# Forgetting recurrence, second quantised feed-forward part and damped recurrence, run as one pipeline over the batches

## The chip, the core and the metric

The kernel runs on one core of one Trainium2 chip. The metric is the device time of that core in microseconds. A core has a matrix engine (TensorE, PE in the profile; its weight loads are the row PEld), a vector engine (VectorE, DVE), an activation engine (ScalarE, ACT), a general engine (GpSimd, POOL) and a queue that issues transfers (SyncE, SP). Each engine works through its own list of instructions in order and waits on semaphores for the others.

## The reference

The residual stream x has 2048 tokens of 128 channels. The whole network is a row of residual parts, `x = x + part(layernorm(x))`; the three that the change touches stand in its middle:

```python
# the forgetting recurrence (batch s of the kernel is one step of the scan, 16 heads of 8)
f = sigmoid(x @ Wf.T + bf);  phi = elu(.) + 1
S = f * S + phi_k (x) v;  z = f * z + phi_k
out = (phi_q . S) / (phi_q . z + 1e-6) @ Wo.T + bo

# the quantised part: blocks of 16 along the last axis are rounded to a 4-bit grid
gate, up = fp4_linear(x, w_gate), fp4_linear(x, w_up)      # 128 -> 352
h = silu(gate) * up
out = fp4_linear(h, w_down)                                # 352 -> 128

# the damped recurrence: a causal filter over the batches, c = gamma * exp(i * theta)
y[n] = real(sum_m c^(n-m) x[m] + last * c^(n+1));  out = y * x
```

Ahead of them stand a latent attention and a first quantised part; behind them four layers of local attention with a gated feed-forward part, two on either side of a gated linear attention.

## The kernel before, in words

The tokens are held in SBUF for the whole run, X (the residual stream) and XH (its normalised copy), as 8 batches (NB) of 2 tiles (NT) of 128 tokens by 128 channels. A plan names the stages in order, `norm0, attn_a, ffn4, forget, ffn4, conv, win, mlp, ...`, and every engine's program walks the plan stage by stage and the batches inside a stage. Semaphores count the events; `v.at(name, i, k)` is the count of event k of batch i in the stage v.

In each stage the last step of a batch on DVE is `residual` (L779: add to X, L782, then the statistics in `norm_stats`, L634), then POOL raises var to the power -1/2 (`rstd_of_batch`, L516 and L518), and DVE writes XH in `norm_apply` (L645).

The recurrence (`forget`): POOL copies XH of the next batch to xst (`stage_copy`, L520), a batch ahead of the rstd that it computes in the same loop (L584 to L591). PE transposes xst (`transpose_x`, L1838), ACT copies the transpose to xT (L1219), PE projects it with a one-row bias matmul and a full one for each tile (`forget_pe`, L1818, banks 0 and 1), ACT takes exp, relu and values out of PSUM (`forget_act`, L1285, signal c_act), and DVE does the step (`forget_step`, L836; L841 is its first instruction, for each tile), whose operands grow with the batch number, since all earlier keys and values are kept and weighted anew. PE transposes the result yC and projects it (`forget_out`, L1826). DVE does step s and then the residual and the normalisation of batch s-1.

The second quantised part (`ffn4`): DVE quantises the hidden values of batch i together with the input of batch i+2 in one interleaved chain (`ffn4_quantise`, L815), PE transposes and multiplies (`ffn4_gates`, L1770, gate and up of both tiles into banks 0 to 3), ACT computes silu (L1272), DVE the product (`ffn4_h`, L826), and PE the down projection (`ffn4`, L1782, bank 7, lines L1788 and L1794). The middle batches are in a hardware loop.

The damped recurrence (`conv`): PE transposes XH (L1801), adds up the taps over all earlier batches in PSUM (`conv_taps`, L1798, banks 0 and 1 in turn), and DVE multiplies by XH and adds to X (`conv_step`, L876). Its end is interleaved with the opening of the first window stage (`win_open`, L921 on DVE), which ends, for this document, at the first instruction of L1576 on PE. POOL clears the buffer keysZ (L514) at the beginning of this stage.

Of the kernel before, what the change touches and what calls it, by code (L numbers as in the profile page):

```python
# [26 lines left out]
P = 128  # L27
NB = 8
# [57 lines left out]
AHEAD = ("forget", "lin")  # L86


def attn_unit(u, groups):


    if u < groups:
# [23 lines left out]
        "stage_ready": 1, "xT_psum": 1, "xT_ready": 1, "c_proj": NT, "c_act": NT, "c_y": 1,  # L116
# [27 lines left out]
             "forget": ["xT_ready", "c_act", "yT_ready", "down_used"], "conv": ["xT_ready", "down_used"],  # L144
# [11 lines left out]
           "pv_done": 2, "o_used": 1, "h_ready": 2, "down_used": 1, "hqT_psum": 1,  # L156
           "shift_done": 16, "p_used": 4, "phi_done": 2, "lin_st": 3, "lin_av": 2, "lin_y": 2}
NAMES = sorted({n for c in COUNTS.values() for n in c})


class Val:


    def __init__(self, sems, plan, at_stage):
        self.sems, self.counts = sems, COUNTS[plan[at_stage]]
        self.base = {n: CREDITS.get(n, 0) + NB * sum(COUNTS[k].get(n, 0) for k in plan[:at_stage])
                     for n in NAMES}

    def at(self, name, i, k):

        assert self.base[name] + k > 0 or (isinstance(i, int) and i * self.counts[name] + self.base[name] + k > 0), (name, k)
        return i * self.counts.get(name, 0) + self.base[name] + k
# [6 lines left out]
class Chain:  # L179
# [6 lines left out]
    def mark(self, ins):  # L186
        self.n += 1
        ins.then_inc(self.val.sems[self.name], 1)
        return self.n

    def wait(self, n):
        self.eng.wait_ge(self.val.sems[self.name], self.val.at(self.name, self.i, n))
# [4 lines left out]
    def close(self, want=None):  # L197
        if want is None:
            want = self.val.counts.get(self.name, 0)
# [3 lines left out]
def build(nc, x, out, consts, w, plan):  # L203
    with ExitStack() as ctx:
# [13 lines left out]
        def carve(name, members):  # L218
# [26 lines left out]
            [("t1", [NT, 2 * FH * FHD]), ("t2", [NT, 2 * FH * FHD]), ("convp", [NT, C])], [("eG", [2, 512]), ("rG", [2, 512]), ("yG", [NT, LH * LHD])]])  # L245
# [21 lines left out]
        hrstd = sb("hrstd", [P, NT])  # L267
        scratch = sb("scratch", [P, 1])
# [18 lines left out]

        ckvZ = tmp["ckvZ"]
# [31 lines left out]
        xhT = tmp["xhT"]; convp = tmp["convp"]  # L320
# [49 lines left out]
        vals = [Val(sems, plan, n) for n in range(len(plan))]  # L370

# [6 lines left out]
        def opens(n):  # L378

            return plan[n] == "conv" and plan[n + 1:n + 2] == ["win"]  # L380

# [22 lines left out]
        def _(sp):  # L404
# [7 lines left out]
            for n, kind in enumerate(plan):  # L412
                if kind == "conv":

                    sp.wait_ge(sems["xh_ready"], vals[n - 2].at("xh_ready", NB - 1, 1))
# [23 lines left out]
        def _(pool):  # L439
# [68 lines left out]
            for n, kind in enumerate(plan):  # L508
# [3 lines left out]
                if kind == "conv":  # L512
# [3 lines left out]
                def rstd_of_batch(i):  # L516
                    pool.wait_ge(sems["var_ready"], v.at("var_ready", i, 1))
                    pool.tensor_tensor(rstd[:], var[:], mhalf[:, 0:NT], ALU.pow).then_inc(sems["rstd_ready"], 1)  # L518

                def stage_copy(i, n=n):  # L520
                    ready = ANNOUNCES.get(plan[n - 1], "xh_ready")
                    pool.wait_ge(sems[ready], vals[n - 1].at(ready, i, 1))
# [45 lines left out]
                if kind == "attn_a":  # L568
# [14 lines left out]
                    continue  # L583
                if kind in AHEAD:  # L584

# [6 lines left out]
                if kind == "win":  # L592

                    pool.wait_ge(sems["xh_ready"], v.before("xh_ready"))
# [20 lines left out]
                if opens(n):  # L615
                    for i in range(2):
                        rstd_of_batch(i)
                    stage_copy(0, n + 1)
                    with pool.Fori(2, NB - 1) as i:
                        rstd_of_batch(i)  # L620
                    inverse_norms(vals[n + 1], 0, 0)
                    rstd_of_batch(NB - 1)
                    continue
# [5 lines left out]
        def _(dve):  # L629
# [4 lines left out]
            def norm_stats(v, i, ch):  # L634

                settle()
                marks = [ch.mark(dve.bn_stats(stats[:, t], X[:, i, t])) for t in range(NT)]
                ch.wait(marks[-1])
                settle()
                for t in range(NT):  # L640
                    m = ch.mark(dve.bn_aggr(mv[:, t], stats[:, t]))
# [1419 lines left out]
```

## Time and profile before

| | |
|---|---|
| median of 3 runs | 2079.46 us (2076.47 to 2080.57) |
| the profiled execution | 2078.81 us, its span 2076.7 us |
| mean granted clock of PE | 0.912 |
| PE busy | 1755.0 us (85%) |
| DVE busy | 1393.1 us (67%) |
| ACT busy | 936.7 us (45%) |
| POOL busy | 453.3 us (22%) |

The span is from the first to the last instruction; the rest of the time lies around it. A share of busy time is a mean over stages that have different limits, so the stretch that the change touches is read by itself. The granted clock is given as a share of 2.4 GHz, and 0.5 is 1.2 GHz. "Idle before" names how long an engine stood and what ended that.

### The profile page before, as it was taken

The numbers are of one execution on the slowest core, as the hardware profiler recorded it, in microseconds if no ns is written. First come the engines' busy times: TensorE is split into PE (matmuls) and PEld (weight loads), VectorE is DVE, ScalarE is ACT, GpSimd is POOL, SyncE is SP. The second block draws the span as 40 slices with busy tenths as digits, with TensorE's granted clock in tenths as the row PEclk, the third lists the DMA queues.
The fourth block names the chain that finished last, engine by engine and source line by source line (L and its number), as shares of the span: only waits on it lengthen the run. The fifth ranks groups of instructions, "written<-read, shape, count | busy, mean of one in ns | idle before, by whom it ended". The sixth has DMA issues, their size and how long they took to land.

```text
span 2076.7 us, 34010 instructions
## 1 busy us (share of the span) xinstructions
PE 1755.0 (85%) x10875; PEld 1415.7 (68%) x10875; DVE 1393.1 (67%) x3623; ACT 936.7 (45%) x2557; POOL 453.3 (22%) x352
## 2 busy tenths in 40 slices
PE   6999986654467699999989789999987999999997
PEld 5888874422246477777777667787775777777776
DVE  4556579646698677787787655566446777777774
ACT  3444432211121456656656445344404566566654
POOL 2200010000001343343343200000003433433440
PEclk9999987655588899999999999999968999999999
DMA  3000000000100000000000000000000000000000
GB/s 138 0 0 0 0 1 0 0 0 0 50 0 1 1 4 3 3 2 3 3 1 3 3 1 0 0 0 0 0 1 0 4 3 3 2 3 3 1 2 23
DMA packets 15104, 13.76 MB, mean 7 GB/s; under 512 B 11286, under 2 KB 14138, under 8 KB 14650
## 3 DMA queue, kind: packets, MB, share of 16 engines
q1 hardware_dynamic: 15034, 12.88, 1.9%
q8 instruction: 37, 0.61, 0.1%
q14 instruction: 33, 0.27, 0.0%
HBM read 9.74 MB, written 1.05 MB: 5 GB/s over the span
## 4 chain that ended last, share of the span: by engine, by line
PE 39%; issue 31%; DVE 24%; ACT 4%; POOL 2%; DVEq 1%; POOLq 0%; ACTq 0%
PE bank L1530 5%; PE bank L1661 3%; DVE arena_ffn L903 3%; DVE arena_attn L918 3%; PE bank L1562 3%; PE bank L1699 3%; DVE ssq L911 3%; PE bank L1550 3%; PE bank L1648 3%; DVE arena_ffn L899 2%; DVE probT L688 2%; PE bank L1724 2%; PE bank L1703 2%; PE bank L1541 2%; DVE nmaxF L681 2%
## 5 line engine op out<-in xcount | busy, mean ns | idle before, releaser
L534 POOL TENSOR_TENSOR arena_ffn<-arena_ffn 128x1024 f32<-128x1024 f32 x60 | 141.3, 2356 | 503.1 <-DVE arena_ffn L903 503.1
L518 POOL TENSOR_TENSOR rstd<-var,mhalf 128x2 f32<-128x2 f32 x48 | 33.4, 695 | 901.2 <-DVE var L643 901.2
L688 DVE COPY probT<-bank 128x512 f32<-128x512 f32 x288 | 196.9, 684 | 25.6 <-PE bank L1541 25.5
L530 POOL TENSOR_TENSOR inv<-ssq,mhalf 128x16 f32<-128x16 f32 x64 | 186.2, 2910 | 69.7 <-DVE ssq L912 69.4
L1550 PE MATMUL bank<-vF,probT 128*128 128x64 f32 x1536 | 195.9, 271 | 5.8 <-DVE probT L688 4.3
L1550 PEld LDWEIGHTS bank<-vF,probT 128*128 128x128 f32 x1536 | 186.5, 192 | 12.8 <-DVE probT L688 12.5
L681 DVE TENSOR_REDUCE nmaxF<-bank 128x2 f32<-128x384 f32 (+1 forms) x192 | 114.8, 598 | 90.1 <-PE bank L1530 89.7
L1530 PE MATMUL bank<-arena_setup 128*128 128x192 f32 (+1 forms) x1024 | 173.0, 302 | 0.0
L1530 PEld LDWEIGHTS bank<-arena_setup 128*128 128x128 f32 x1024 | 155.8, 193 | 12.5 <-issue 1.1
L1371 ACT ACTIVATE arena_conv<-bank,nmaxF 128x192 f32<-128x192 f32 x256 | 105.4, 419 | 115.9 <-DVE nmaxF L681 112.5
L1253 ACT ACTIVATE prob<-bank,nmax 128x128 f32<-128x128 f32 (+1 forms) x256 | 88.7, 428 | 125.0 <-DVE nmax L681 125.0
L1562 PE MATMUL bank<-packF,hT 128*128 128x512 f32 x256 | 123.3, 606 | 1.8 <-ACT hT L1305 1.8
L681 DVE TENSOR_REDUCE nmax<-bank 128x2 f32<-128x512 f32 (+1 forms) x96 | 65.1, 689 | 66.2 <-PE bank L1530 66.2
L1661 PE MATMUL bank<-xT,w1s 128*114 128x256 f32 (+1 forms) x384 | 103.8, 397 | 3.3 <-ACT xT L1352 1.1
L1330 ACT ACTIVATE arena_setup<-bank 128x512 f32<-128x512 f32 x64 | 38.1, 595 | 151.2 <-PE bank L1610 150.7
L1541 PE MATMUL bank<-ident,prob 128*128 128x128 f32 x640 | 96.8, 274 | 9.4 <-ACT prob L1253 9.3
L1310 ACT ACTIVATE arena_attn<-bank 128x512 f32<-128x512 f32 x128 | 69.6, 601 | 74.6 <-PE bank L1562 74.6
L1054 DVE TENSOR_TENSOR arena_forget<-bank,maskG 128x384 f32<-128x384 f32 x128 | 68.2, 552 | 50.4 <-PE bank L1726 47.4
L1530 PE MATMUL bank<-arena_attn 128*128 128x256 f32 (+1 forms) x512 | 99.3, 326 | 0.0
L1219 ACT ACTIVATE xT<-bank 128x256 f32<-128x256 f32 x40 | 15.3, 383 | 183.9 <-PE bank L1841 130.2
L903 DVE TENSOR_TENSOR arena_ffn<-bank,rope 128x256 f32<-128x256 f32 x256 | 95.5, 415 | 0.0
L1576 PE MATMUL bank<-packF,hT 128*128 128x512 f32 x128 | 73.6, 662 | 24.5 <-DVE arena_ffn L903 24.5
(257 smaller groups left out, 4262.4 us busy)
## 6 DMA issues: line engine op xcount, KB each, us to landing
packF<-in_packF SPq DMA_DIRECT2D x1, 3122.0 KB
arena_history<-in_packG SPq DMA_DIRECT2D x1, 2560.0 KB, 9.1
HS<-XH SPq DMA_DIRECT2D x32, 63.5 KB
X<-in_x_tiled SPq DMA_DIRECT2D x1, 1024.0 KB, 4.9
out_dram<-X SPq DMA_DIRECT2D x8, 128.0 KB, 1.9
arena_setup<-in_const_masks_a SPq DMA_DIRECT2D x1, 512.0 KB, 5.4
arena_setup<-in_const_masks_f SPq DMA_DIRECT2D x1, 512.0 KB
HS<-XH SPq DMA_DIRECT2D x32, 0.2 KB
```

The lines of the kernel that those rows point to most:

```text
L530: pool.tensor_tensor(inv[:, t, :, 0], ssq[:, t, :, 0], mhalf[:, 0:16], ALU.pow).then_inc(sems["inv_ready"], 1)
L534: pool.tensor_tensor(t1[:, t], t1[:, t], t2[:, t], ALU.add).then_inc(sems["rope_sum"], 1)
L681: dve.tensor_reduce(out_[:, u, 0:heads], bank[u % banks][:, 0:heads * keys].rearrange("p (h k) -> p h k", k=keys), AX.X, ALU.max, negate=T ...
L688: dve.tensor_copy(probT[:, u % 2], bank[4 + u % 2][:]).then_inc(sems["pt_copied"], 1)
L903: ins = dve.tensor_tensor(heads(t2[:, t, cols])[:, :, d], a[:, :, e], tab, ALU.mult)
L1253: ins = act.activation(prob[:, u % 2, m * keys:(m + 1) * keys], bank[u % 4][:, m * keys:(m + 1) * keys], ACT.Exp, bias=nmax[:, u, m:m + 1])
L1371: ins = act.activation((prob, probW)[t][:, u % 2, (k + 1) * keys - width:(k + 1) * keys], bank[u % F_SCORE_BANKS][:, k * width:(k + 1) * w ...
L1530: ins = pe.matmul(bank[s % banks][:, n * width:(n + 1) * width], q, k, start=False, stop=True, skip_group_check=True)
L1541: ins = pe.transpose(bank[4 + u % 2][:, n * P:(n + 1) * P], pr[:, u % 2, n * P:(n + 1) * P], ident[:])
L1550: ins = pe.matmul(o, probT[:, u % 2, n * P:(n + 1) * P], val, start=first, stop=(kt == keys // P - 1), skip_group_check=True)
L1562: ins = pe.matmul(bank[banks[m]][:], hT[:, t * P:(t + 1) * P], f_at[f"wqkv{l}"][:, 512 * m:512 * m + 512], start=True, stop=True)
L1661: return pe.matmul(dst, w1s[:, l, lo:lo + n], xT[:], start=True, stop=True)
```

## The change

The three stages `forget`, `ffn4` (the second one) and `conv` become one loop of NB+3 turns, written out, on each engine. In turn k the recurrence works on batch k, the quantised part (now called `q`, with its own semaphores) quantises the hidden values of batch k-2 together with the input of batch k-1, and the damped recurrence does batch k-3. PE and ACT do the projections of the recurrence one batch ahead (k+1). Each of the three has its own tiles for the statistics (the table `moments`). PE transposes XH itself, without POOL's copy. The PSUM banks are shared out anew: 0 and 1 projections, 2 both transposes of the recurrence (by halves), 3 the taps, 4 the transposes of q and conv (by halves), 5 and 6 gate, then up in the same bank after silu has read it, and the transposes of hq, 7 the two outputs (by halves). ACT changes between the tables of Exp and Silu in every turn (`prime`). The memset of keysZ moves to the beginning of `forget`. The core of the diff:

```diff
-AHEAD = ("forget", "lin")
+AHEAD = ("lin",)
-    plan = ["norm0", "attn_a", "ffn4", "forget", "ffn4", "conv"] + local + ["lin"] + local
+    plan = ["norm0", "attn_a", "ffn4", "forget", "q", "conv"] + local + ["lin"] + local
...
 # POOL
+                if kind == "forget":
+                    vq, vc = vals[n + 1:n + 3]
+                    for k in range(NB + 3):
+                        if k < NB:
+                            rstd_of_batch(k)
+                        if k == NB + 2:
+                            inverse_norms(vals[n + 3], 0, 0)
+                        if inside(k - 3) is not None:
+                            rstd_of_batch(k - 3, vc)
+                        if k == NB:
+                            stage_copy(0, n + 3)
+                        if inside(k - 2) is not None:
+                            rstd_of_batch(k - 2, vq)
+                    continue
...
 # DVE
+                    for k in range(NB + 4):
+                        if k < NB:
+                            forget_step(vf, k)
+                        q_quantise(vq, vf, inside(k - 2), inside(k - 1))
+                        if k < NB:
+                            forget_end(vf, k)
+                        if k == NB + 2:
+                            win_open(vals[n + 3], 0, 0)
+                        if inside(k - 3) is not None:
+                            conv_step(vc, k - 3)
+                        if inside(k - 2) is not None:
+                            q_end(vq, k - 2)
+                        if k < NB:
+                            norm_apply(vf, k)
+                        if inside(k - 3) is not None:
+                            norm_apply(vc, k - 3)
+                        if inside(k - 2) is not None:
+                            norm_apply(vq, k - 2)
+                        if inside(k - 1) is not None:
+                            q_h(vq, k - 1)
+                    win_open(vals[n + 3], 0, 1)
...
 # ACT
+                    forget_act(v, 0)
+                    for k in range(NB + 3):
+                        if inside(k - 3) is not None:
+                            take_tokens(vc, k - 3)
+                        if k + 1 < NB:
+                            forget_act(v, k + 1)
+                        if k < NB:
+                            forget_yT(v, k)
+                        if inside(k - 2) is not None:
+                            q_hqT(vq, k - 2)
+                        if inside(k - 1) is not None:
+                            prime(ACT.Silu)
+                            q_take_xT(vq, k - 1)
+                            q_silu(vq, k - 1)
+                            prime(ACT.Exp, 1)
+                    win_open(vals[n + 3])
...
 # PE
+            def q_out(v, i, vf):
+                pe.wait_ge(v.sem("hq_ready"), v.at("hq_ready", i, 1))
+                for t in range(NT):
+                    for n in range(NCH):
+                        ins = pe.transpose(bank[5 + t][:, n * P:(n + 1) * P], hq[:, t, n * P:(n + 1) * P], ident[:])
+                    ins.then_inc(v.sem("hqT_psum"), 1)
+                if i + 2 < NB:
+
+                    pe.wait_ge(vf.sem("down_used"), vf.at("down_used", i + 2, 1))
+                elif i:
+                    pe.wait_ge(v.sem("down_used"), v.at("down_used", i, 0))
...
+            def q_gates(v, i):
+                pe.wait_ge(v.sem("xq_ready"), v.at("xq_ready", i, 1))
+                for t in range(NT):
+                    ins = pe.transpose(bank[4][:, t * P:(t + 1) * P], xq[:, t * P:(t + 1) * P], ident[:])
+                ins.then_inc(v.sem("xT_psum"), 1)
+                pe.wait_ge(v.sem("xT_ready"), v.at("xT_ready", i, 1))
+                for m, done in enumerate(("gate_ready", "up_ready")):
+                    for t in range(NT):
+                        if m:
+                            pe.wait_ge(v.sem("silu_ready"), v.at("silu_ready", i, t + 1))
+                        pe.matmul(bank[5 + t][:, 0:FI], xqT[:, t * P:(t + 1) * P], wguT[:, m, 0:FI], start=True,
+                                  stop=True).then_inc(v.sem(done), 1)
...
+                    forget_pe(v, 0, vals[n - 1])
+                    for k in range(NB + 3):
+                        if inside(k - 3) is not None:
+                            conv_taps(vc, k - 3, vq)
+                        if k + 1 < NB:
+                            forget_pe(v, k + 1, vals[n - 1])
+                        if k < NB:
+                            forget_out(v, k)
+                        if inside(k - 2) is not None:
+                            q_out(vq, k - 2, v)
+                        if inside(k - 1) is not None:
+                            q_gates(vq, k - 1)
+                    win_open(vals[n + 3], 0)
```

In `forget_pe` and `forget_out` the first bias matmul now stands ahead of the wait for ACT's copy.

## Rows read from the trace of the kernel before

**Rows 1.** Windows: time, then busy of PE, PEld, DVE, ACT, POOL; clock, DMA.
```profile
397.00:555.90 158.90, 85.01 (x160) 37.78 (x160) 89.57 (x217) 21.04 (x81) 8.33 (x16) 0.50 0.00 0
555.90:652.70 96.80, 59.27 (x230) 42.72 (x230) 88.80 (x264) 20.05 (x49) 4.85 (x7) 0.76 0.07 27
...
397.00:691.80 294.80, 169.63 (x587) 102.99 (x587) 206.99 (x588) 46.84 (x143) 28.33 (x38) 0.64 0.02 9
```

**Rows 2.** Waits of DVE from 397.0 to 691.8: total us, times, longest.
```profile
DVE arena_forget L841 <- ACT cEf L1295: 57.9, 16, 5.2
DVE XH L649 <- POOL rstd L518: 9.7, 12, 0.8
```

**Rows 3.** Timeline (start, us, engine, line), last step of the recurrence.
```profile
526.59 0.48 PE L1840 MATMUL bank<-ident,xst 128*128 128x128 f32 x1 [11.82 <-POOL xst L526]
...
532.05 0.29 DVE L841 SCALAR_TENSOR_TENSOR arena_forget<-arena_forget 128x128 f32<-128x128 f32 x1 [5.18 <-ACT cEf L1295]
...
535.32 0.29 DVE L841 SCALAR_TENSOR_TENSOR arena_forget<-arena_forget 128x128 f32<-128x128 f32 x1 [2.68 <-ACT cEf L1295]
...
549.17 0.41 DVE L782 TENSOR_TENSOR X<-X,bank 128x256 f32<-128x256 f32 x1
549.31 0.69 PE L1829 MATMUL bank<-ident,arena_forget 128*128 128x128 f32 x2 [10.74 <-DVE arena_forget L867]
...
553.47 0.42 DVE L782 TENSOR_TENSOR X<-X,bank 128x256 f32<-128x256 f32 x1 [1.46 <-PE bank L1835]
```

**Rows 4.** Timeline, seam into the recurrence and its second step.
```profile
394.77 0.42 DVE L782 TENSOR_TENSOR X<-X,bank 128x256 f32<-128x256 f32 x1 [1.81 <-PE bank L1794]
...
397.47 0.31 PE L1840 MATMUL bank<-ident,xst 128*128 128x128 f32 x1 [2.73 <-POOL xst L526]
...
402.61 0.29 DVE L841 SCALAR_TENSOR_TENSOR arena_forget<-arena_forget 128x128 f32<-128x128 f32 x1 [4.95 <-ACT cEf L1295]
...
413.73 0.29 DVE L841 SCALAR_TENSOR_TENSOR arena_forget<-arena_forget 128x128 f32<-128x128 f32 x1 [2.68 <-ACT cEf L1295]
...
419.06 0.42 DVE L782 TENSOR_TENSOR X<-X,bank 128x256 f32<-128x256 f32 x1
```

**Rows 5.** Timeline, two turns of the second quantised part.
```profile
619.89 0.89 DVE L725 TENSOR_REDUCE amax<-arena_ffn 128x44 f32<-128x704 f32 x1
...
621.47 2.63 PE L1779 MATMUL bank<-wguT,xT 128*128 128x352 f32 x8 [0.56 <-ACT xT L1219]
...
627.82 0.42 DVE L782 TENSOR_TENSOR X<-X,bank 128x256 f32 x1
...
629.10 2.93 PE L1794 MATMUL bank<-wdT,arena_ffn 128*128 128x128 f32 x12
...
630.66 0.88 DVE L725 TENSOR_REDUCE amax<-arena_ffn 128x44 f32<-128x704 f32 x1
...
633.02 4.78 PE L1779 MATMUL bank<-wguT,xT 128*128 128x352 f32 x8 [0.56 <-ACT xT L1219]
...
637.26 0.41 DVE L782 TENSOR_TENSOR X<-X,bank 128x256 f32<-128x256 f32 x1
```

**Rows 6.** Timeline, damped recurrence and opening of the window stage.
```profile
653.38 1.81 POOL L514 MEMSET arena_setup<- 128x2048 f32 x1
...
655.26 0.40 DVE L880 TENSOR_TENSOR arena_ffn<-bank,XH 128x256 f32<-128x256 f32 x1
...
657.04 0.42 DVE L880 TENSOR_TENSOR arena_ffn<-bank,XH 128x256 f32<-128x256 f32 x1
...
670.09 0.38 PE L1801 MATMUL bank<-ident,XH 128*128 128x128 f32 x2
...
674.22 0.14 PEld L1840 LDWEIGHTS bank<-ident,xst 128*128 128x128 f32 x1
...
691.79 1.19 PE L1576 MATMUL bank<-packF,hT 128*128 128x512 f32 x1 [12.53 <-DVE arena_ffn L903]
```

**Rows 7.** ACT's table loads by line: busy us, mean ns, idle before.
```profile
L1266 ACT ACT_TABLE_LOAD x58 | 74.4, 1283 | 1.0
```

More of the change, by code:

```diff
@@ L829, in ffn4_h, with q_h, q_quantise, q_end @@
                     dve.tensor_tensor(h[:, t], silu[:, t], bank[2 * t + 1][:, 0:FI], ALU.mult).then_inc(sems["h_ready"], 1)
+            def q_h(v, i):
+                for t in range(NT):
+                    dve.wait_ge(v.sem("up_ready"), v.at("up_ready", i, t + 1))
+                    dve.tensor_tensor(h[:, t], silu[:, t], bank[5 + t][:, 0:FI], ALU.mult).then_inc(v.sem("h_ready"), 1)
+            def q_quantise(v, vin, hi, xi):
+                jobs = ([h_job(v, hi)] if hi is not None else []) + ([x_job(v, xi, vin)] if xi is not None else [])
+                if not jobs:
+                    return
+                ch = Chain(dve, v, "quant_chain", 0, q_quantise.links)
+                last = quantise(jobs, ch.mark, ch.wait)
+                q_quantise.links = ch.n
+                if xi is not None:
+                    last.pop().then_inc(v.sem("xq_ready"), 1)
+                if hi is not None:
+                    last.pop().then_inc(v.sem("hq_ready"), 1)
+            q_quantise.links = 0
+            def q_end(v, i):
+                ch = Chain(dve, v, "dve_chain", i)
+                residual(v, i, ch, bank[7][:, 0:T])
+                ch.close()
             def ffn4_end(v, i):
@@ L1298, in forget_yT @@
                 act.wait_ge(sems["yT_psum"], v.at("yT_psum", s, 1))
-                act.activation(yT[:], bank[2][:, 0:T], ACT.Copy).then_inc(sems["yT_ready"], 1)
+                act.activation(yT[:], bank[2][:, T:2 * T], ACT.Copy).then_inc(sems["yT_ready"], 1)
             def shifted(v, i, b=2):
@@ L1796, in ffn4 @@
                 ins.then_inc(sems["down_ready"], 1)
+            def q_out(v, i, vf):
+                pe.wait_ge(v.sem("hq_ready"), v.at("hq_ready", i, 1))
+                for t in range(NT):
+                    for n in range(NCH):
[5 more added lines that the diff above has]
+                    pe.wait_ge(v.sem("down_used"), v.at("down_used", i, 0))
+                for t in range(NT):
+                    pe.wait_ge(v.sem("hqT_ready"), v.at("hqT_ready", i, t + 1))
+                    for n in range(NCH):
+                        ins = pe.matmul(bank[7][:, t * P:(t + 1) * P], hqT[:, t, n], wdT[:, n],
+                                        start=(n == 0), stop=(n == NCH - 1))
+                ins.then_inc(v.sem("down_ready"), 1)
@@ L1807, in conv_taps @@
+                ins.then_inc(v.sem("xT_psum"), 1)
+                if i:
+                    pe.wait_ge(v.sem("down_used"), v.at("down_used", i, 0))
+                y = bank[3]
                 for t in range(NT):
@@ L1902, in _ @@
                 v = vals[n]
-                if kind.startswith("mlp") or kind == "win" and not begins(n):
+                if kind.startswith("mlp") or kind in ("q", "conv") or kind == "win" and not begins(n):
                     continue
```

195 lines of the change are left out of this document (93 added, 102 removed).

## The prediction

> **What bounds the kernel now.** I read the page first, then the stretch that the change touches as windows [rows 1], then what VectorE (DVE) waits for in it [rows 2], then one turn of each of the three stages as a timeline. The stretch runs from 397.0 to 691.8 us: 294.8 us, of which DVE is busy 207.0 and PE 169.6. No engine is full. In the forgetting recurrence (158.9 us) DVE is busy 89.6, and in the quantised part (96.8 us) 88.8 [rows 1]: the second is bound by DVE, the first by a wait. That wait has one row: DVE stood 57.9 us, 16 times, before L841, for the last of ScalarE's (ACT) reads of the projections [rows 2]. The timeline says why. The transposes of batch 7 start at 526.59, after 11.82 us of waiting for GpSimd's (POOL) copy xst, though XH of that batch is far older: the copy stands in POOL's queue behind the square root of batch 5. L841 then starts 5.46 us later for the first half and 3.27 us later again for the second [rows 3]. The other waits are 9.7 us for POOL's rstd [rows 2] and single stalls at the seams. PE is granted half of its clock (1.2 GHz) through the whole recurrence, 0.76 on average in the quantised part [rows 1].
>
> **The change, part by part.** I follow DVE, because in the new order each engine's queue is a fixed list of turns k, and DVE has the most work. Its turn is: recurrence step k, joint quantisation (hidden of batch k-2, input of k-1), residual of the recurrence k, damped step k-3, residual of the quantised part k-2, three normalisations, gating products k-1.
>
> Prices. (a) Recurrence step: batch 1 from 413.73 to 419.06 [rows 4], batch 7 from 535.32 to 549.17 [rows 3], each plus 0.59 for its first half: 5.9 and 14.4, growing by 1.42 a batch, so 58.0 for batches 3 to 7 and 7.3 for batch 2. (b) Joint quantisation: 619.89 to 627.82, 7.9. Hidden alone: 630.66 to 637.26, 6.6 [rows 5]. (c) Residual with statistics 1.45 (its six instructions follow one another), damped step 655.26 to 657.04, 1.8 [rows 6]; one normalisation 0.53; gating products 0.95. (d) rstd on POOL 0.9 with its hop: it stalled 12 times for 9.7 [rows 2].
>
> Removed: POOL's copy and its semaphore on the path to the transposes; PE now transposes XH itself, and the projections of k+1 are issued a turn ahead, during step k. So the 57.9 us should shrink to the first batch. They need PE for about 1.3 us and four matmul groups of 1.63 (two of them are the 3.27 us of rows 3), 7.9 us at half clock, behind the taps of k-3. A step is 8.8 us or more from k=3 on and PE starts 0.6 us before it, so the taps of batch 0 (six matmuls, about 2 us) and the projections end at about the time the step ends; the later, longer taps meet longer steps. What queues behind them is the output of the recurrence. That one takes 4.2 us from the last product to the residual (549.25 to 553.47 [rows 3]), 3.6 now that its bias matmul goes ahead of ACT's copy, and it lies beside the 7.9 us of quantisation. Late next is therefore not L841 but the end of the turn.
>
> Let T be the end of the joint quantisation. DVE's own work after it is 1.45+1.8+1.45+1.6+0.95, so the turn could end at T+7.2. But the quantised part's output needs PE: after the quantisation ended at 627.82 its down projection ran from 629.10 for 2.93 us at the lower clock [rows 5], so the residual can start at T+4.3, where DVE would be at T+3.25. PE's gates k-1 stand behind it: transposes and ACT's copy, 0.9 us at full clock or 1.3 at half (5.46 less 3.27 less 0.9 for ACT's reads), then four matmuls of 352 columns, 2.63 us at full clock or 4.78 at half [rows 5], 0.3 for hops and the silu, 0.5 for the last product. That gives T+8.6 with the projection at the lower clock and the gates at the higher one, T+7.2 all high (then DVE itself is the bound), T+11.2 all low. I take 8.6: after a down projection at the lower clock the gates ran in 2.63 us four times of five in the trace, in 4.78 once; one of each stands in [rows 5].
>
> Added on ACT: a table load before each Silu and before each Exp of the next turn, 17 instead of 2. One takes 1.28 us, and 58 of them elsewhere in this kernel had 1.0 us of idle time before them in all [rows 7]. Silu's load runs from about T+1.9 to T+3.4 (T+1.2 to T+2.7 at full clock), and the transposes that it must not delay end at T+5.2 or T+3.3. Exp's load lies beside taps and transposes. I cost them at nothing; if the cover were gone, one load per turn is 1.28 x 8 = 10 us. The Trainium skill, ScalarE: Activation LUTs, "What ACT_TABLE_LOAD costs", adds a drain of 1380 ns to 1283 ns per switch, and its section on table sets advises to batch calls by set, which speaks against this change; with 2.66 us in each of eight turns the sum would be 21 us worse. The trace agrees with the 1283 ns, not with a drain.
>
> Moved at no cost: the memset of keysZ, 1.81 us on POOL [rows 6], now at the start of the stretch, where DVE waits anyway (it can lengthen one normalisation beside it that nobody waits for). SP's load of packG is issued when the recurrence's last batch is normalised, as before, and is needed stages later. The unrolled q turns replace loops; nothing in the trace prices that, and the recurrence, already unrolled, shows no fetch stall, so zero, bounds -3 to +3 us.
>
> **The sum**, in times of the trace before.
> - k=0: PE waited for xst until 397.47; the residual that it must wait for ends at 395.2 [rows 4]. The first L841 moves from 402.6 to 400.4, the second half to 403.7, the step ends at 407.6. The projections of batch 1 (four groups, 6.5) stand ahead of output 0: 410.2, output 413.8, residual, rstd, normalisation: 416.7.
> - k=1: +5.9 = 422.6; output 3.6 = 426.2 (input quantisation, 16 blocks of 60, is shorter); gates at half clock 1.3+4.8+0.3+0.5 = 433.1.
> - k=2: +7.3+7.9+8.6 = 456.9.
> - k=3 to 7: 58.0+5x16.5 = 597.6.
> - k=8: 16.5 = 614.1. k=9: 6.6, then down projection 4.5, residual 1.45, rstd 0.9, normalisation 0.5 = 628.1.
> - Tail: the taps of batch 7 now start only here: 670.09 to 674.22 is 4.1 us at full clock [rows 6], 8.2 at half, I take 5.5. From 674.22 to 691.79 the opening of the window stage is unchanged, 17.6 us. Ends at 651.3.
> That is 40.5 us earlier than 691.8. The profiled execution took 2078.8 us (span 2076.7 and 2.1 around it), 0.7 below the median of the three; 2078.8-40.5 = 2038.3.
>
> **The rivals.**
> - PE stays at half clock, as in the whole recurrence before [rows 1], whose bursts of 7 us did not lift it: 2.6 us more in k=2 to 8, 4 us in the tail: +22, 2060. For it: the same projections, with one-row bias matmuls, are in every turn. Against: the clock rose in the quantised part with less PE work per time.
> - PE at full clock through: -1.4 in seven turns, -3 in k=1, -3 in k=9 and tail: -16, 2022. Against it: PE idles from the output k to T.
> - The table loads are in the chain: +10 us by the row, 2049, up to 2060 where two stand in a turn. By the page's price it would be 2059.
> - Slower than before: the in-order queues expose what I hide. If step k+1 found its projections not done (8.7 us from transposes to the second L841 [rows 3]) and output k was exposed too (3.6), a turn costs 12.3 more, seven turns 86: 2124. It decides from half of the turns on (40.5/12.3 = 3.3). It would take PE's queue running a turn behind DVE's; in my sum PE is ahead by only a fraction of a microsecond at k=3.
> - It doesn't do what it says: smaller new waits (POOL, bank 7 shared by two outputs, gates) of 5 to 6 us in each of seven turns eat the gain: about 2078.
>
> **How the numbers follow.** Chances: forecast 0.50 (2029 to 2048), half clock 0.20, full clock 0.15, table loads 0.05, slower 0.06, no change 0.04. The range 2018 to 2066 takes the first four with the bounds of the unrolled code and of clock changes in later stages (some us either way). Faster 0.90, within 0.2% (4 us, about what a measurement of this kernel can tell from no change) 0.03, slower 0.07.
>
> **What would show it.** Right: L841's idle time under 10 us; L782 of the quantised part waiting about 1 us a turn for the down projection and the last product about 0.3 us for PE; turns from k=3 of 25 to 31 us; the window stage unchanged, 40 us earlier. Wrong: idle time before L841 from k=2 on, the recurrence's residual waiting in turns after k=1, ACT's loads naming themselves as releasers, or a stretch in which DVE is busy under 75%.

## The result and the profile after

The changed kernel took 2022.28 us (median of four runs, 2020.02 to 2022.44), the kernel before, in runs on the same chip, 2080.02 us (2076.47 to 2084.73). The ratio is 0.9719, with an interval of 0.9698 to 0.9739: 58 us faster, where 40.5 was forecast. The profiled execution took 2022.21 us (span 2020.4), 56.6 less than the one of before.

Of these I first look for the part that lies in the stretch. Windows of the kernel after (time, then busy of PE, PEld, DVE, ACT, POOL; clock, DMA): the whole stretch, up to the first instruction of L1656, which was L1576.

```profile
395.00:645.90 250.90, 155.69 (x586) 100.42 (x587) 204.90 (x596) 68.87 (x167) 26.38 (x31) 0.70 0.03 11
```

The kernel before, from 395.00 as well ([rows 1] starts it at 397.00):

```profile
395.00:691.80 296.80, 169.63 (x587) 102.99 (x587) 208.08 (x596) 46.84 (x143) 29.05 (x39) 0.64 0.02 9
```

DVE runs 596 instructions in both. They keep it busy for 208.08 of 296.80 us (70%) before and for 204.90 of 250.90 us (82%) after. The stretch ends 45.9 us earlier (645.9 against 691.8; forecast 651.3).

Waits of DVE from 395 to 645.9, kernel after (total us, times, longest). L894 was L841, L811 was L782, L678 was L649; L1892 is the down projection of q, L1952 the output of the recurrence, L1906 the gates.

```profile
DVE X L811 <- PE bank L1892: 12.3, 8, 2.9
DVE ssq L961 <- ACT arena_attn L1383: 10.4, 1, 10.4
DVE X L811 <- PE bank L1952: 6.0, 1, 6.0
DVE arena_ffn L863 <- PE bank L1906: 3.3, 4, 2.0
DVE XH L678 <- POOL rstd L539: 2.4, 3, 0.8
DVE arena_forget L894 <- ACT cEf L1368: 2.3, 1, 2.3
```

The row of 57.9 us in [rows 2] has become one of 2.3. In its place stand the down projection of the quantised part (eight waits, 12.3 us) and one wait for the output of the recurrence in the first turn.

A turn in the middle shows where these lie. Timeline of the kernel after (start, us, engine, line), from the last part of recurrence step 6 (turn k=6) to the start of step 7:

```profile
544.99 0.88 DVE L754 TENSOR_REDUCE amax<-arena_ffn 128x44 f32<-128x704 f32 x1
...
546.46 0.80 PE L1952 MATMUL bank<-woTb,yT 128*128 128x128 f32 x2
...
552.70 1.54 PE L1882 MATMUL bank<-ident,hq 128*128 128x128 f32 x6 [3.99 <-DVE hq L802]
552.90 0.41 DVE L811 TENSOR_TENSOR X<-X,bank 128x256 f32<-128x256 f32 x1
...
554.27 2.90 PE L1892 MATMUL bank<-wdT,arena_ffn 128*128 128x128 f32 x12
...
554.79 1.28 ACT L1339 ACT_TABLE_LOAD   x1
...
556.08 0.20 ACT L1339 ACTIVATE primer<-mhalf 128x1 f32<-128x1 f32 x1
...
557.21 0.42 DVE L811 TENSOR_TENSOR X<-X,bank 128x256 f32<-128x256 f32 x1 [1.09 <-PE bank L1892]
...
558.07 3.03 PE L1906 MATMUL bank<-wguT,xqT 128*128 128x352 f32 x8 [0.47 <-ACT xqT L1281]
...
560.20 1.28 ACT L1339 ACT_TABLE_LOAD   x1
560.54 1.11 DVE L863 TENSOR_TENSOR arena_ffn<-arena_ffn,bank 128x352 f32<-128x352 f32 x2 [0.37 <-PE bank L1906]
561.57 0.28 DVE L894 SCALAR_TENSOR_TENSOR arena_forget<-arena_forget 128x128 f32<-128x128 f32 x1
```

The joint quantisation starts at 544.99 and the recurrence's residual follows it at 552.90 without a wait; its output on PE was done long before. From there to the next step (561.57) DVE waits 1.09 us for the down projection and 0.37 us for the last gate product. Both table loads lie beside PE's work and nobody names them. The other turns from k=3 to k=7 look alike; the wait for the down projection is 0.51 us in turn 3 and 0.91 to 1.10 us in turns 4 to 7. It is longer in turn 2 (2.89 us) and where DVE has less to do beside it, in turns 8 and 9 (2.42 and 2.33 us).

The stretch gives 45.9 us and the whole 56.3 (spans). The other 10.4 lie far behind it. I cut both spans at the same instructions: the start of the last batch of gated linear attention (first score matmul, L1724 before, L1804 after) and its last output matmul (L1766, L1846).

| part of the span, us | before | after | difference |
|---|---|---|---|
| to the end of the stretch | 691.8 | 645.9 | -45.9 |
| window stages and gated linear attention, up to its last batch | 815.35 | 821.59 | +6.2 |
| last batch of gated linear attention | 42.85 | 30.21 | -12.6 |
| the rest | 526.7 | 522.7 | -4.0 |

The windows of that batch, before and after:

```profile
1507.00:1550.00 43.00, 39.52 (x209) 35.48 (x209) 19.04 (x74) 2.35 (x4) 0.69 (x1) 0.60 0.00 1
```
```profile
1467.00:1498.00 31.00, 26.73 (x214) 23.90 (x212) 18.94 (x74) 2.39 (x4) 0.70 (x1) 0.94 0.01 1
```

The same instructions (74 on DVE in both), and PE at a mean clock of 0.60 in one and 0.94 in the other. The change doesn't touch the source of this batch. The timeline of before shows where the clock fell; the same group of four takes 0.70 us at first and 1.23 in the last row:

```profile
1507.15 0.70 PE L1724 MATMUL bank<-arena_setup 64*128 64x256 f32 x4
...
1509.51 0.70 PE L1724 MATMUL bank<-arena_setup 64*128 64x256 f32 x4 [1.43 <-DVE arena_forget L1054]
...
1511.08 0.52 PE L1747 MATMUL bank<-vG,arena_forget 128*128 128x65 f32 x2
...
1512.38 1.23 PE L1724 MATMUL bank<-arena_setup 64*128 64x256 f32 x4
```

It falls from 2.4 to 1.2 GHz at about 1511, 1.6 us after the end of a hole of 1.43 us, and stays there for 34 us, in which PE is busy 96% of the time:

```profile
1511.00:1545.00 34.00, 32.64 (x154) 29.36 (x153) 15.65 (x62) 1.19 (x2) 0.00 (x0) 0.50 0.00 1
```

In the kernel after the same hole is there (1.43 us, ending at 1469.84), and the groups behind it still take 0.70 us.

### The profile page after: what moved, and what is told of

Its sections match the earlier page's. It is cut to its first block, busy times and chain, and to the rows that moved or that the text cites. A ratio compares the mean times of both kernels' runs of the same rounds, so it can differ in the third digit from the quotient of the medians.

```text
span 2020.4 us, 33580 instructions
## 1 busy us (share of the span) xinstructions
PE 1724.9 (85%) x10818; PEld 1403.6 (69%) x10875; DVE 1389.0 (69%) x3623; ACT 957.3 (47%) x2580; POOL 450.6 (22%) x344
## 4 chain that ended last, share of the span: by engine, by line
PE 43%; DVE 33%; issue 18%; ACT 4%; POOL 1%; DVEq 1%; POOLq 0%; ACTq 0%
PE bank L1610 5%; PE bank L1741 4%; DVE arena_ffn L953 3%; DVE arena_attn L968 3%; PE bank L1779 3%; PE bank L1642 3%; DVE ssq L961 3%; PE bank L1728 3%; PE bank L1630 3%; DVE arena_ffn L949 3%; DVE probT L717 2%; PE bank L1783 2%; PE bank L1804 2%; DVE nmaxF L710 2%; PE bank L1621 2%
## 5 line engine op out<-in xcount | busy, mean ns | idle before, releaser
L539 POOL TENSOR_TENSOR rstd<-var,mhalf 128x2 f32<-128x2 f32 x32 | 22.3, 696 | 796.5 <-DVE var L672 796.5
L1610 PEld LDWEIGHTS bank<-arena_setup 128*128 128x128 f32 x1024 | 154.3, 191 | 12.3 <-issue 1.0
L1339 ACT ACT_TABLE_LOAD x74 | 94.9, 1283 | 1.3
L1656 PE MATMUL bank<-packF,hT 128*128 128x512 f32 x128 | 73.3, 659 | 25.1 <-DVE arena_ffn L953 25.1
```

The costliest lines, as they stand in the source:

```text
L1339: act.activation(primer[:, col:col + 1], mhalf[:, 0:1], func)
L1610: ins = pe.matmul(bank[s % banks][:, n * width:(n + 1) * width], q, k, start=False, stop=True, skip_group_check=True)
```

## The experiments

Two questions are open: what in the stretch brought the 45.9 us, the pipeline or a part of it; and whether the other 10 us belong to the change. "Stretch end" and "batch" below are the first and third row of the table above, for the profiled execution. The same code of the stretch, profiled again in a kernel that differs only behind it, ended it at 691.5 to 691.8 in the order of before (before, e5, e10), at 644.1 to 646.1 in the changed order (after, e6, e11), at 644.2 and 645.1 in e1 and e7, and at 636.5 and 634.6 in e4 and e8. So a difference of up to 2 us between two stretch ends is not read as an effect.

**e1: the copy alone.** The kernel before, three stages one after the other, with PE transposing XH itself in `forget`:

```diff
-AHEAD = ("forget", "lin")
+AHEAD = ("lin",)
...
-            def forget_pe(v, s):
-                transpose_stage(v, s, bank[6])
+            def forget_pe(v, s, vin):
+                pe.wait_ge(sems["xh_ready"], vin.at("xh_ready", s, 1))
+                for t in range(NT):
+                    ins = pe.transpose(bank[6][:, t * P:(t + 1) * P], XH[:, s, t], ident[:])
+                ins.then_inc(sems["xT_psum"], 1)
+                pe.wait_ge(sems["xT_ready"], v.at("xT_ready", s, 1))
...
```

> The kernel before with one edit: TensorE transposes XH itself in the recurrence, without GpSimd's copy; the three stages still follow one another. Theory A (the copy behind the square root is what cost the time, and the pipeline over the three stages adds little): the projections of batch s+1 stand behind output s-1 and take 4.2 + 8.7 = 13 us from the last product of s-1, VectorE's step s and its residual take 8.8 to 17 us, so waits of about 4, 3 and 1 us stay at the first steps, some 16 us before L841 in all instead of 57.9; the stretch takes 250 to 255 us instead of 294.8, the kernel 2036 to 2040. Theory B (the pipeline is what hides them): L841 still waits 30 us or more, the kernel takes 2050 or more.

Measured: 2031.44 us, ratio 0.9783 (0.9767 to 0.9799). Theory A holds, with more gain than it gave: L841 waits 11.5 us where 16 were expected, and the time is 5 us below its range. Windows of the recurrence and of the stretch, and DVE's waits:

```profile
397.00:555.00 158.00, 109.01 (x261) 55.85 (x260) 131.29 (x344) 30.70 (x105) 6.93 (x10) 0.58 0.05 17
397.00:644.20 247.20, 165.27 (x584) 101.67 (x583) 205.87 (x588) 45.94 (x142) 25.51 (x30) 0.66 0.03 11
```
```profile
DVE arena_forget L841 <- ACT cEf L1295: 11.5, 7, 2.7
DVE XH L649 <- POOL rstd L518: 9.7, 12, 0.8
DVE ssq L911 <- ACT arena_attn L1310: 6.0, 1, 6.0
DVE arena_ffn L829 <- ACT arena_ffn L1272: 2.6, 2, 1.6
```

The stretch ends at 644.2, that of the whole pipeline at 645.9: the same within the scatter. The order of before already issues the projections of batch s+1 ahead of the output of batch s; only POOL's copy, queued behind an older rstd, held them back. The trace of before shows it ahead of the last step:

```profile
525.50 0.69 POOL L518 TENSOR_TENSOR rstd<-var,mhalf 128x2 f32<-128x2 f32 x1 [22.77 <-DVE var L643]
526.14 0.40 POOL L526 COPY xst<-XH 128x256 f32 x1
```

POOL stood idle for 22.77 us, waiting for the statistics of batch 5; the copy of batch 7, 0.40 us long, stood behind it, though its input had been there for nearly all of that time. With it gone, DVE is busy 131.29 of 158.00 us (83%) in the recurrence, against 89.57 of 158.90 (56%) in [rows 1], with the stages still one after the other. The pipeline hides more of the rstd (9.7 becomes 4.2 in all) and of the projections (11.5 becomes 2.3), and pays with the down projection (12.3), the first output (6.0) and a longer wait at the seam into the window stage (10.4 for 6.0).

**e2: projections in their own turn.** The changed kernel, but in turn k PE and ACT do the projections of batch k, not k+1:

```diff
-                    forget_pe(v, 0, vals[n - 1])
...
-                        if k + 1 < NB:
-                            forget_pe(v, k + 1, vals[n - 1])
+                        if k < NB:
+                            forget_pe(v, k, vals[n - 1])
```

(the same for `forget_act`).

> The changed kernel with the recurrence's projections and ScalarE's reads of them in the turn of their batch instead of one turn ahead. By the price of the rival in the prediction (12.3 us a turn, seven turns at half clock) 86 us more, 2108; if TensorE holds its full clock behind the gates and the taps, 5 us for the projections and the taps of 2 to 3 us ahead of them, 8 us a turn, 55 more, 2077. If running ahead were of no use: 2022.

Measured: 2070.3 us (2050.84 to 2076.8), ratio 0.9942 (0.991 to 0.9974); stretch end 682.3, 36.4 later than in the changed kernel.

```profile
DVE arena_forget L894 <- ACT cEf L1368: 39.6, 15, 5.3
```

This row is 37.3 us more than the 2.3 of before the edit. The first output waits 2.3 us less (3.7 for 6.0) and the seam 1.0 us more (11.4 for 10.4), so this one wait explains the 36.4 us. In this profile the pipeline without the projections run ahead keeps 9.5 of the 45.9 us. The eight runs scatter over 26 us and the profiled one is the slowest of them, so another run may have kept more; even the fastest is only 26 us below the kernel before on its chip, where the changed kernel is 58 us below. The expectation of 86 us at the lower clock was too high; the one of 55 us more, at the full clock (2077), is near the profiled 2076.8. But that total has 12.6 us of the later batch in it, and the stretch had 36.4. So what carries most of the gain is that the projections are issued during the step ahead, in either order.

**e3: no table changes.** Silu replaced by a plain copy and both `prime` calls left out in the loop, so that the part computes gate times up, not silu(gate) times up, with 16 table loads fewer.

```diff
-                    act.activation(silu[:, t], bank[5 + t][:, 0:FI], ACT.Silu).then_inc(v.sem("silu_ready"), 1)
+                    act.activation(silu[:, t], bank[5 + t][:, 0:FI], ACT.Copy).then_inc(v.sem("silu_ready"), 1)
...
-                            prime(ACT.Silu)
...
-                            prime(ACT.Exp, 1)
```

> The changed kernel with Silu replaced by a plain copy and both table changes of each turn left out: the quantised part computes gate * up instead of silu(gate) * up, everything else is as it was, and 16 table loads of 1.28 us are gone. Loads hidden, as in the sum of the prediction: 2020 to 2023, no change. Loads in the chain (one or two a turn): 10 to 21 us faster, 2001 to 2012.

Loads by line (busy us, mean ns, idle before), first the changed kernel, then this one:

```profile
L1339 ACT ACT_TABLE_LOAD x74 | 94.9, 1283 | 1.3
```
```profile
L1339 ACT ACT_TABLE_LOAD x58 | 74.4, 1283 | 1.0
```

Measured: stretch end 645.7 against 645.9. Without sixteen loads, 20.5 us of ACT's time, the stretch ends 0.2 us sooner, which is inside the scatter of 2 us, where the rival had 10 to 21 us: they are hidden. The Trainium skill's page ScalarE: Activation LUTs, section "What ACT_TABLE_LOAD costs", has 1283 ns for the load, as here; its drain of 1380 ns on top, which was a rival, shows in no row: in the turn above the load ends at 556.07 and ACT's next instruction starts at 556.08. And yet the time was 2035.73 us (2035.7, 2035.76, 2037.02, and one of 2021.32), 13 us slower than the changed kernel. Of the 13.6 us between the profiled spans 12.6 are the batch of gated linear attention:

```profile
1465.00:1508.00 43.00, 39.52 (x210) 35.47 (x209) 19.03 (x74) 2.32 (x4) 0.70 (x1) 0.60 0.00 1
```

It took 42.84 us here, as before the change, and in e1 42.86. Two kernels whose stretches end within 0.2 us of each other differ by 12.6 us in a batch 800 us later. That answers half of the second question: the pipeline alone does not bring those us, since e3 has it and runs this batch at the lower clock (so does e2, at a mean of 0.60).

**e4: a higher clock in the pipeline.** Matmuls whose result nobody reads (256 columns, into bank 4), on PE while it waits for the recurrence step or for the quantisation:

```diff
+            def fill(n):
+                for _ in range(n):
+                    pe.matmul(bank[4][:, 0:T], ident[:], wC[:, 0:T], start=True, stop=True)
...
+                        if 3 <= k < NB:
+                            fill((6, 8, 10, 12, 20)[k - 3])
                         if k < NB:
                             forget_out(v, k)
+                        if k > 2 and inside(k - 2) is not None:
+                            fill(6)
                         if inside(k - 2) is not None:
                             q_out(vq, k - 2, v)
```

> The changed kernel with idle TensorE time filled by matmuls of 256 columns whose result nobody reads: 6 to 20 of them while the recurrence's step runs on VectorE (turns 3 to 7) and 6 between its output and that of the quantised part. If the lower clock of the down projection costs about 1.1 us a turn (the wait before the residual), that wait goes and turns 3 to 9 get 1 to 1.5 us shorter: 2012 to 2016. If VectorE is the bound anyway: 2022. If the fillers run at the lower clock they stand in the way, 1 us each instead of 0.5: 2025 to 2040.

```profile
395.00:636.50 241.50, 189.88 (x783) 128.24 (x783) 203.78 (x596) 68.33 (x167) 26.42 (x31) 0.82 0.03 12
```

The clock of the stretch rose from 0.70 to 0.82 and its end moved from 645.9 to 636.5. The 9.4 us lie in what the expectation had for seven shorter turns (7 to 10.5). The time is 2017.87 us in the median, but the four runs are two pairs, 2009 and 2027 to 2028; the profiled one is a 2009, and its batch ran at a mean clock of 0.89 (from 1453 to 1485). A comparison to a few us needed the later batch to be held still.

**e5 to e8: the batch held at the higher clock.** Three such matmuls in the last batch of gated linear attention, early in it, where PE otherwise falls to half:

```diff
+                    if not more and s == 2:
+                        pe.wait_ge(sems["p_used"], v.at("p_used", i, 16))
+                        for _ in range(3):
+                            pe.matmul(bank[0][:, 0:T], ident[:], wC[:, 0:T], start=True, stop=True)
```

in the kernel before (e5), the changed one (e6), e1 (e7) and e4 (e8), all on one chip, where the kernel before took 2080.80 us.

> The kernel before with three matmuls of 256 columns (result read by nobody, 1.5 us at full clock) in the 1.4 us in which TensorE waits between the first and the second pair of heads of the last batch of the gated linear attention. In the trace before, that batch took 42.9 us at the lower clock, in the trace after 30.2 us at the full one. Theory C (10 of the 56 us of the change were this batch's clock, which falls or not in that hole, and have nothing to do with the pipeline): the batch takes 30 to 31 us, the kernel 2063 to 2066 in every run instead of 2076. Theory D (the clock there follows from something else, the hole isn't its cause): 2076 to 2081 as before.

> The changed kernel with the same three matmuls. Theory C: the batch had kept its clock there already in this kernel's runs, so nothing changes: 2020 to 2024, and the gain against the kernel before with the same matmuls is the 45.9 us of the stretch alone, or less. Theory D: the difference stays at 56 us.

> The three stages one after another, TensorE transposing XH itself (one edit to the kernel before), with the same three matmuls. Its stretch ended at 644.2, that of the changed kernel at 645.9, but its last batch of the gated linear attention took 42.9 us. Theory C: 2031.4 less 12 = 2019 to 2020, as fast as the whole pipeline with the hold or 1 to 2 us faster. Theory D: 2031 as before.

> The changed kernel with filled TensorE time in the pipeline's turns (its runs fell into 2009 and 2027) and the same three matmuls. Theory C: all runs at about 2009, the fastest version so far. Theory D: two groups again, 2009 and 2027.

| kernel with the hold | us, median | ratio to before | stretch end | batch |
|---|---|---|---|---|
| e5, before | 2071.73 | 0.996 (0.9941 to 0.9979) | 691.5 | 32.6 |
| e6, changed | 2025.42 | 0.9719 (0.9693 to 0.9744) | 646.1 | 30.4 |
| e7, copy alone | 2022.86 | 0.9713 (0.9692 to 0.9734) | 645.1 | 32.7 |
| e8, changed with fillers | 2013.35 | 0.9669 (0.965 to 0.9689) | 634.6 | 30.4 |

Three matmuls take 10 us off that batch in the kernel before, and 9 off its time:

```profile
1510.00:1543.00 33.00, 30.04 (x215) 26.95 (x214) 19.03 (x75) 2.39 (x4) 0.70 (x1) 0.84 0.00 1
```

The mean clock is 0.84, so the batch is held for the most part, not throughout; theory C had 30 to 31 us and 2063 to 2066. In e7 the hold takes 10.2 us off the batch as well (42.86 to 32.7). In e8 it leaves the batch at 30.4, and the four runs lie within 6.8 us, not in two pairs 18 us apart, though 3 to 10 us above the 2009 that was expected. With the hold, before and changed differ by 46.3 us (2071.73 less 2025.42): the stretch is 45.4 of it in the profiles, the batch 2.2, and the rest of the span gives 2.0 back. The pipeline and the copy alone can't be told apart (their intervals overlap). The fillers make the pipeline 12 us faster, and e8 is the fastest kernel of the study, ahead of both given ones.

**e9: fillers in the sequential order.** e7 with the 56 fillers of the recurrence, ahead of the outputs of batches 3 to 7.

```diff
+                        if s > 3:
+                            fill((6, 8, 10, 12, 20)[s - 4])
                         if s:
                             forget_out(v, s - 1)
```

> The three stages one after the other, without POOL's copy, with the same filler matmuls in the recurrence (6, 8, 10, 12, 20 ahead of the outputs of batches 3 to 7) and the same three in the last batch of gated linear attention. Theory A, that the pipeline gives no more than the removed copy: the fillers bring the sequential order as much as they brought the pipeline (9 us in the stretch), which then ends at 635 to 639 in the profile, the time 2012 to 2017 us. Theory B, that a faster PE is worth something only in the pipeline, whose turns end in PE's gates, while a step of the sequential recurrence ends with VectorE: the stretch ends at 642 to 646, the time 2019 to 2024 us.

```profile
397.00:555.00 158.00, 126.18 (x372) 75.26 (x370) 132.18 (x345) 30.86 (x105) 6.95 (x10) 0.71 0.05 17
```

Measured: 2026.16 us (2023.09 to 2030.4), ratio 0.974 (0.9717 to 0.9762); stretch end 642.8, against 645.1 in e7. The clock of the recurrence rose from 0.58 (e1) to 0.71, for 2.3 us, little more than the scatter of the stretch; the time is no better than e7's. Theory B holds for the stretch, though its time was put 2 us too low. DVE stood 12.4 us at L841 (11.5 in e1). That wait falls in the first four steps, ahead of the first filler, so this run doesn't show what a faster PE would make of it. There PE had little idle time to fill:

```profile
408.00:450.00 42.00, 37.57 (x79) 18.86 (x77) 31.33 (x90) 8.70 (x35) 2.08 (x3) 0.52 0.00 0
```

It is busy 89% of these 42 us, at nearly the lower clock, and whether it would catch up with a higher one stays open. In the pipeline the rows that did shrink are these (e8; L1896 is the down projection, L1960 the output):

```profile
DVE X L811 <- PE bank L1896: 5.9, 3, 2.9
DVE X L811 <- PE bank L1960: 5.4, 1, 5.4
```

The down projection cost 12.3 us in eight waits and now 5.9 in three. So of the orders that were built, the pipeline is ahead only with fillers: by 8.2 us in the stretch (642.8 less 634.6), with ratios of 0.9669 and 0.974 whose intervals don't touch. The two don't have the same fillers, though: e8 has 98, of which 42 stand ahead of the quantised part's outputs, and e9 only the 56 of the recurrence. Fillers in the quantised part of the sequential order were not tried. DVE is idle for 8.0 us in that part (96.80 less 88.80, [rows 1]), and with the 12.4 us at L841 that leaves room for the whole difference; that no filling of the sequential order reaches e8 is not shown.

**e10 and e11: does a shift in time flip the batch?** One more instruction of DVE (a maximum over 1640 values, about 1.8 us, used by nobody) in the first window stage, in the kernel before and the changed one:

```diff
+                    if n == 6:
+                        dve.tensor_reduce(idle[:], packF[:, 0:DELAY], AX.X, ALU.max)
```

> The kernel before, with one VectorE instruction of about 1.8 us more that nothing uses (a maximum over 1640 values) in the first window stage, some 600 us ahead of the last batch of gated linear attention. Theory of the state (that batch runs at the lower clock or not by where it happens to start, and any shift can turn it): the batch takes 30 to 33 us in at least one of this run and the next where it took 42.9 and 30.2 before, or the reverse, with the total moved by 9 to 12 us and not by 1.8. Rival (the clock follows from the work that the pipeline changes): the batch stays at 42.9 us here and the time is 2080 to 2083 us.

> The changed kernel with the same 1.8 us instruction of VectorE in the first window stage. Theory of the state: the last batch of gated linear attention may fall to 42.9 us, and the time is then 2034 to 2037 us; if it stays at 30.2 it is 2022 to 2025. Rival (the pipeline itself raised the clock there): the batch stays at 30.2 us and the time is 2022 to 2025 us.

Measured: e10 2084.99 us, ratio 1.0018 (1.0001 to 1.0035), batch 42.81; e11 2027.22 (two runs of 2020 and 2023, two of 2031.28), batch 31.02 in the profiled 2020.43. Neither batch changed its level in the profile, so that a small shift flips it is not shown. Nor does its start decide: it took 31.02 us from 1464.58 (e11) and 42.84 from 1465.56 (e3), 42.86 from 1466.14 (e1) and 30.21 from 1467.49 (after). What sets the level stays open. Of the profiles without the hold, the three of the sequential order (before, e1, e10) all have the lower level, and of the five of the pipeline two have it (e2, e3) and three the higher one (after, e4, e11); so a part that the order plays is not excluded either. The totals suggest that the level differs between runs of one kernel too: e3 has one run 14 us below its others, e11 has two runs 8 to 11 us above its other two, and one run of before, beside e9 to e11, took 2068.1 where the other twelve took 2080 to 2086. These runs have no trace, only a mean clock (0.916 against 0.907 to 0.911 for that run of before).

## Why the prediction was right or wrong

The direction, the mechanism and the range held; the forecast of 2038.3 us was 16 us above the measured 2022.28. Step by step, in times of the trace (turns 0 to 6 end at the next start of L894, turns 7 and 8 with DVE's last product, turn 9 with its last normalisation):

| step | forecast | measured |
|---|---|---|
| second half of step 0 starts | 403.7 | 401.74 |
| end of turn 0 | 416.7 | 414.66 |
| turn 1 | 16.4 | 15.4 |
| turn 2 | 23.8 | 23.3 |
| turns 3 to 7 | 140.7 | 139.1 |
| turn 8 | 16.5 | 16.9 |
| turn 9 | 14.0 | 13.6 |
| tail | 23.2 | 23.0 |
| stretch end | 651.3 | 645.9 |

The forecasts are the recorded ones. Their own terms add up to 140.5 for turns 3 to 7 (58.0 and five times 16.5) and to a stretch end 0.2 to 0.3 us sooner; that is a slip in the sum, too small to matter.

- **The stall of 57.9 us shrinks to the first batch**: right, 2.3 us once.
- **Turn = step + 7.9 + 8.6**: right. In the turn shown above the quantisation ends at 552.98, the quantised part's residual starts at T+4.23 (forecast 4.3) and the turn ends at T+8.6; the five turns from k=3 have 7.7 to 8.7. They take 24.5 to 30.9 us, where 25 to 31 was named as a sign of being right, and DVE is busy 82% of the stretch, where under 75% was a sign of being wrong. PE was mixed as assumed: down projection 2.90 us (lower clock), gates 3.03.
- **Turn 0** was 2 us too long in my sum. This term was mis-sized: I had priced its projections at the lower clock, as in the recurrence of before. But they now start 1.8 us sooner behind the down projections of the stage ahead, and the clock has not yet fallen when the first ones run (first group 0.94 us, second 1.70):

```profile
395.63 0.41 PE L1932 MATMUL bank<-ident,XH 128*128 128x128 f32 x2 [0.82 <-DVE X L811]
...
396.84 0.94 PE L1940 MATMUL bank<-wC,xT 128*128 128x400 f32 x2
...
398.87 0.27 DVE L894 SCALAR_TENSOR_TENSOR arena_forget<-arena_forget 128x128 f32<-128x128 f32 x1
399.06 1.70 PE L1940 MATMUL bank<-wC,xT 128*128 128x400 f32 x2
...
401.74 0.29 DVE L894 SCALAR_TENSOR_TENSOR arena_forget<-arena_forget 128x128 f32<-128x128 f32 x1 [2.31 <-ACT cEf L1368]
```

  The first half of step 0 came at 398.87, not 400.4. In e1, which has no bias matmuls ahead of ACT's copy, the halves start at 399.08 and 401.76: reordering these matmuls gave nearly nothing here, the earlier start did. Turn 1 (1.0 us), turn 2 (0.5) and turns 3 to 7 (1.6) make up the rest of the 5.4 us by which the stretch ended sooner than forecast; turns 8, 9 and the tail nearly cancel.
- **Table loads at nothing**: right, 0.2 us by e3, with a scatter of 2 us.
- **Memset moved, on POOL**: right in that nobody waited long. A normalisation of DVE got longer beside it:

```profile
397.00 1.80 POOL L534 MEMSET arena_setup<- 128x2048 f32 x1
397.09 1.79 DVE L678 TENSOR_SCALAR XH<-X,mv,rstd 128x128 f32<-128x128 f32 x1 [0.81 <-POOL rstd L539]
```

  It took 1.79 us instead of 0.34 and ended at 398.88, as the first L894 starts. The memset of before, at the start of the damped recurrence ([rows 6]), had done the same:

```profile
653.48 1.79 DVE L649 TENSOR_SCALAR XH<-X,mv,rstd 128x128 f32<-128x128 f32 x1 [0.81 <-POOL rstd L518]
```

  There DVE's next product followed at 655.26 without a wait. So the move spared DVE about 1.4 us there (an estimate, 1.79 less 0.34), a small gain that the sum had at nothing.
- **What failed: the term that was not there.** The sum stopped at the window stage and took the rest as unchanged, and the range had "clock changes in later stages (some us either way)". What it put at nothing gave 10.4 us, and one batch alone moved by 12.6. With it and the 4.0 us of the rest, less the 6.2 of the middle, the remaining 10.4 us are accounted for (5.4 + 10.4 is the error of 15.8 in the profiled spans). The middle is scatter: it lies between 815.4 and 825.0 us in the thirteen profiles, with no order by kernel (818.5 in e5 and 821.9 in e10, whose code up to there is that of before but for the one instruction of e10). The batch has two levels, 30 to 31 and 42.8 us, and [rows 1] could not show it, since I looked at no window behind the stretch. A mean clock of 0.60 over 43 us in which PE is busy 92% of the time was to be seen in the trace of before, and its price too: the same group of four takes 1.23 us at the lower clock and 0.70 at the higher one.
- **The rival with full clock** gave 2022, the measured time, but for a reason that didn't occur: the stretch ran at 0.70. The time agrees by chance.
- **The attribution to the pipeline was too generous.** The sum was right for the order as it stands, but a single edit inside it, the copy, is enough for all of it (e1, e7). The prediction had read the cause rightly, the copy behind the square root of an older batch, and did not ask what removing it alone would give.

## What to carry to other kernels

Before stages are merged to fill an engine's idle time, name the one queue entry that makes it idle and move that alone: here a copy of one engine, queued behind an older rstd, was worth the whole pipeline. A pipeline moves the ends of the turn to another engine, and may then be worth only what that engine's clock allows: raise the clock in both versions, in all their stages, before comparing them. When kernels are compared to within 1%, cut the spans at equal instructions first, since a batch far away can have two levels 12 us apart, and profile the same code more than once, since the end of one stretch moved by up to 2 us by itself.

## What the runs showed of the hardware

- In the last batch of gated linear attention of the kernel before, the granted clock fell about 1.6 us after a hole of 1.43 us and stayed at 1.2 GHz for 34 us, with PE busy 96% of that time. The same code ran at a mean of 0.94 in the kernel after, with a hole of the same length at the same place. Three matmuls of 256 columns put in early brought it to 0.84 and 32.6 us.
- In the recurrence of the sequential order PE ran at a mean of 0.58 (e1); with 56 more matmuls of 256 columns beside the steps (e9) at 0.71.
- A DVE tensor_scalar that takes 0.34 us took 1.79 beside a memset of 1.80 or 1.81 us on POOL, in the kernel before at 653.48 and in the one after at 397.09; both times it ended within 0.1 us of the memset. Beside a copy of 0.40 us on POOL, at 526.14, it took 0.39.
- The 74 table loads of ScalarE at L1339 took 1283 ns in the mean, with 1.3 us of idle time before them in all; in the turn shown the next instruction followed 0.01 us behind the load.
